# A mixture-of-experts kernel: the experts' second matrix laid out and loaded as 96 rows instead of 88

## The chip, the cores and the metric

The kernel runs on one core of a Trainium2 chip. The metric is the time of one launch on the device, in microseconds (us), the median of several runs. The core has a matrix engine (PE; its weight loads are shown apart as PEld), a vector engine (DVE), a scalar engine (ACT), a general engine (POOL), an engine that here only issues DMA transfers (SP), and 16 DMA engines that carry all transfers.

## What is computed

Two layers, each attention and then a feed-forward part, with a layer norm after each, over 2 x 1024 tokens of 256 features in fp32. The change touches only the last part, a mixture of experts. Cut to this part, the reference is:

```
E, I, K = (64, 176, 6)
router_logits = x @ gate_w.T
probs = jax.nn.softmax(router_logits, axis=-1)
topk_w, topk_idx = jax.lax.top_k(probs, K)
topk_w = topk_w / jnp.sum(topk_w, axis=-1, keepdims=True)
combine = jnp.sum(jax.nn.one_hot(topk_idx, E, dtype=x.dtype) * topk_w[..., None], axis=1)
h = jax.nn.silu(jnp.einsum('th,eih->tei', x, experts_w1))
y = jnp.einsum('tei,ehi->teh', h, experts_w2)
routed_out = jnp.einsum('teh,te->th', y, combine)
```

A shared expert is added to `routed_out`, and the layer norm closes the kernel. Every token goes to 6 of 64 experts. Each expert has a first matrix of 256 x 176 and a second of 176 x 256.

## The kernel before

The routed work is sorted by expert: 2048 x 6 = 12288 rows, in 96 tiles of 128 rows (FULL). A tile may hold rows of several experts, so the loop of `experts` runs over 159 pairs of a tile and an expert (STEPS = 96 + 63). The router (`route`) works out, on the chip, the token of every row (`tok_i`), its place in the output (`dst_i`), and the expert and tile of each step (`owner`).

Step b does the following:

- SP loads the expert's number with a value load (L1848), waits until the step five earlier has finished with the buffer (`y_made`), and issues two transfers: the first matrix into `w1` (L1850), 128 rows of 1408 bytes, and the second into `w2` (L1851), 88 rows of 2048 bytes. There are B = 5 buffers of each. The profile calls the buffers `moe_w`; two of the five `w2` lie in a tile named `keep_prod`, and show under that name.
- POOL gathers the rows of tile b + 6 from memory (L1869, as long as there are tiles), and from step 64 on scatters a finished tile of outputs (L1874). Both are indirect transfers of 128 rows of 1 KB.
- PE transposes a gathered tile (`turn`, L1901), multiplies it by the first matrix (`up`, L1912: eight matmul instructions a step), and multiplies the result of the step before by the second (`down`, L1921: four instructions).
- ACT copies the transposed tile (L1952, L1960) and applies SiLU to the first product (L1966), and DVE adds the second product to the tile's sum under a mask (L2010).

The second product has an inner size of 2 x 88. It is taken as 2 x 96 (HPAD): PE reads 96 rows of `ht` (the SiLU's result) and of `w2`, and the rows 88 to 95 of both must hold zeros. POOL therefore clears the two `ht` and the five `w2` buffers once, in the router's stage (L1603), and counts them on the semaphore `padded`; SP waits for all seven clears ahead of its first weight load (L1560), PE and ACT at the start of the experts stage. Each transfer then writes rows 0 to 87 only.

The first five steps' matrices are loaded in the router's stage (L1563, L1565), as soon as SP has fetched the list of experts. At the end of the kernel the outputs are read back from memory, weighed and added up, and normalised.

In memory, `lay_out` stores each expert's second matrix as 88 rows of 512 floats (the two halves of the inner dimension side by side).

Of the kernel before, what the change touches and what calls it, by code (L numbers as in the profile page):

```python
# [19 lines left out]
KT = E // P  # L20
# [1432 lines left out]
HALF = WIDE // 2  # L1453
HPAD = 96
# [8 lines left out]
B, RB, LEAD = 5, 9, 6  # L1463
# [6 lines left out]
def route(nc, a, keep):  # L1470


    with ExitStack() as ctx:
# [75 lines left out]
        @block.sync  # L1549
        def _(sp):  # L1550
            sp.dma_start(w_up[:], a["w_sh_up"].rearrange("(k p) n -> p k n", p=P)).then_inc(sh_in, 16)
            for m, width in enumerate(SH_TILES):
                sp.dma_start(w_down[0:width, m], a["w_sh_down"][m * P:m * P + width]).then_inc(sh_in, 16)
            sp.dma_start(a["x_rows"].rearrange("(t p) n -> p t n", p=P), x[:]).then_inc(x_out, 16)
            sp.wait_ge(owned, 1)
            sp.dma_start(a["owners"].rearrange("(j p a) -> p j a", p=P, j=2), owner_i[:]).then_inc(owner_out, 16)
            sp.wait_ge(owner_out, 16)
            sp.dma_start(owner[:], a["owners"].rearrange("(o n) -> o n", o=1)).then_inc(owner_in, 16)
            sp.wait_ge(owner_in, 16)
            sp.wait_ge(keep["padded"], 2 + B)  # L1560
            for b in range(B):
                e = sp.value_load(owner[0:1, b:b + 1], min_val=0, max_val=EXPERTS - 1)
                sp.dma_start(keep["w1"][b][:], a["w1"][e].rearrange("p (k j n) -> p k j n", k=KT, j=2)  # L1563
                             ).then_inc(keep["w_in"][b], 16)
                sp.dma_start(keep["w2"][b][0:HALF], a["w2"][e].rearrange("p (j n) -> p j n", j=2)  # L1565
                             ).then_inc(keep["w_in"][b], 16)
            sp.wait_ge(x_out, 16)

        @block.gpsimd
        def _(pool):  # L1570
            done = 0

            def ordered(instruction):

                nonlocal done
                instruction.then_inc(consts, 1)
                done += 1
                pool.wait_ge(consts, done)

            ordered(pool.iota(iota[:], pattern=[[1, TILES]], base=0, channel_multiplier=0,  # L1580
                              allow_small_or_imprecise_dtypes=True))
            ordered(pool.iota(lane[:], pattern=[[1, 1]], base=0, channel_multiplier=1,
                              allow_small_or_imprecise_dtypes=True))
            ordered(pool.iota(tile_no[:], pattern=[[1, 2]], base=0, channel_multiplier=2,
                              allow_small_or_imprecise_dtypes=True))
            ordered(pool.memset(ones[:], 1.0))
            ordered(pool.memset(ones_f[:], 1.0))
            ordered(pool.memset(zeros[:], 0.0))
            ordered(pool.iota(token[:], pattern=[[P, NT]], base=1, channel_multiplier=1,
                              allow_small_or_imprecise_dtypes=True))  # L1590
            ordered(pool.iota(k_rows[:], pattern=[[TOK, TOP - 1]], base=0, channel_multiplier=0,
                              allow_small_or_imprecise_dtypes=True))
            ordered(pool.memset(before[:], 1.0))
            ordered(pool.memset(below[:], 1.0))
            ordered(pool.affine_select(out=before[:], in_=before[:], compare_op=ALU.is_gt, fill=0.0,
                                       base=0, pattern=[[1, P]], channel_multiplier=-1))
            ordered(pool.affine_select(out=below[:, 0], in_=below[:, 0], compare_op=ALU.is_gt, fill=0.0,
                                       base=0, pattern=[[1, EXPERTS]], channel_multiplier=-1))
            ordered(pool.affine_select(out=below[:, 1], in_=below[:, 1], compare_op=ALU.is_ge, fill=0.0,
                                       base=0, pattern=[[1, EXPERTS]], channel_multiplier=-1))  # L1600
            ordered(pool.memset(sums[:, 0], 0.0))
            for m in keep["ht"] + keep["w2"]:
                pool.memset(m[:], 0.0).then_inc(keep["padded"], 1)  # L1603
            for n in range(UNITS):
                width = SH_TILES[n % ST]
                pool.wait_ge(silu, n + 1)
                pool.wait_ge(u_in, n + 1)
                pool.tensor_tensor(sh_h[n // ST][0:width, n % ST], sh_gate[n % 2][0:width], sh_up[n % 2][0:width],
                                   ALU.mult).then_inc(fuse, 1)
            pool.wait_ge(split, 1)  # L1610
            for n, (t, k) in list(enumerate(pairs))[1::2]:
                if n >= HOTS:
                    pool.wait_ge(hot_used, n - HOTS + 1)
                pool.tensor_scalar(hot_low[:, n % HOTS], iota[:, 0:P], low[:, t, k:k + 1], None,
                                   ALU.is_equal).then_inc(hot_low_in, 1)
            pool.wait_ge(x_out, 16)
            pool.wait_ge(tok_in, 1)
            for t in range(LEAD):
                pool.indirect_dma_start(keep["rows"][t], None, a["x_rows"], bass.IndirectOffsetOnAxis(
                    ap=tok_i[:, t:t + 1], axis=0)).then_inc(keep["rows_in"][t], 16)  # L1620
# [186 lines left out]
def experts(nc, a, keep):  # L1807

    with ExitStack() as ctx:
# [4 lines left out]
        w1, w2, rows_all, rows, ht = (keep[n] for n in ("w1", "w2", "rows_all", "rows", "ht"))  # L1814
        w_in, rows_in, padded = (keep[n] for n in ("w_in", "rows_in", "padded"))
# [28 lines left out]
        @block.sync  # L1844
        def _(sp):
            for b in range(B, STEPS):
                n = b % B
                e = sp.value_load(owner[0:1, b:b + 1], min_val=0, max_val=EXPERTS - 1)  # L1848
                sp.wait_ge(y_made, b - B + 1)
                sp.dma_start(w1[n][:], a["w1"][e].rearrange("p (k j n) -> p k j n", k=KT, j=2)).then_inc(w_in[n], 16)  # L1850
                sp.dma_start(w2[n][0:HALF], a["w2"][e].rearrange("p (j n) -> p j n", j=2)).then_inc(w_in[n], 16)  # L1851
            for n in range(B):
                sp.wait_ge(w_in[n], 32 * len(range(n, STEPS, B)))
            sp.wait_ge(xt_in, STEPS)
            for n in range(YB):
                sp.wait_ge(y_out[n], 16 * len(range(n, FULL, YB)))
            for t in range(NT):
                sp.dma_start(got[t], a["y_rows"].rearrange("(k t p) n -> t p k n", k=TOP, p=P)[t]).then_inc(got_in[t], 16)
            for a0, a1 in NORM:
                sp.wait_ge(norm["normed"], a1)  # L1860
                sp.dma_start(a["out"].rearrange("(t p) n -> p t n", p=P)[:, a0:a1], x[:, a0:a1]).then_inc(stored, 16)
            sp.wait_ge(stored, 16 * len(NORM))
# [28 lines left out]

        @block.tensor
        def _(pe):
            pe.wait_ge(padded, 2 + B)

            def turn(t):
                pe.wait_ge(rows_in[t % RB], 16 * (t // RB + 1))
# [49 lines left out]
        def _(act):  # L1947
            def keep_tile(t):
                act.wait_ge(turned, t + 1)
                if t >= RING:  # L1950
                    act.wait_ge(xt_in, t - RING + EXPERTS)
                act.activation(tiles[:, t % RING], xt_ps[t % 2][:, 0:KT * P].rearrange("p (k t) -> p k t", k=KT),  # L1952
                               ACT.Copy).then_inc(tile_in, 1)
# [12 lines left out]
                act.activation(ht[b % 2][0:HALF], h_ps[b % 2][0:HALF, 0:2 * P].rearrange(  # L1966
                    "p (j t) -> p j t", j=2), ACT.Silu).then_inc(h_in, 1)

            act.wait_ge(padded, 2 + B)
            keep_tile(0)  # L1970
            take_tile(0)
            keep_tile(1)
# [140 lines left out]
def lay_out(i):  # L2113
# [3 lines left out]
    d = {}  # L2117
# [13 lines left out]
    for n, k in enumerate(("w_q1", "w_k1", "w_v1")):  # L2131
# [6 lines left out]
    w1, w2 = t(np.asarray(i["L1_ffn_experts_w1"])), t(np.asarray(i["L1_ffn_experts_w2"]))  # L2138
    rows = lambda w, k: np.ascontiguousarray(w.reshape(EXPERTS, k, w.shape[1] // k, w.shape[2]).transpose(
        0, 2, 1, 3).reshape(EXPERTS, w.shape[1] // k, k * w.shape[2]))  # L2140
    d["w1"], d["w2"] = rows(w1, KT), rows(w2, 2)
    d["w_sh_up"], d["w_sh_down"] = t(np.asarray(i["L1_ffn_shared_gate_up"])), t(np.asarray(i["L1_ffn_shared_down"]))
    return d

# [23 lines left out]
```

## Time and profile before

| | |
|---|---|
| median of 3 runs | 1293.59 us (1291.06 to 1298.01) |
| the profiled execution | 1297.3 us, its span 1295.6 us |
| PE busy | 1128.8 us (87% of the span) |
| DVE, ACT, POOL busy | 825.3, 633.3, 592.2 us |
| DMA | 137.21 MB, a mean of 106 GB/s |
| expert loop | from 910 to 1239 us |

PE's busy share alone says little here: the profile also shows what each engine waited for, the chain of waits that ended last, and, for any stretch, the mean busy share of the 16 DMA engines and the rate that they moved. A mean share below 1 can come from 16 engines that are all partly idle, or from some that are full beside others that are empty.

### The profile page before, as it was taken

To read this page: it belongs to the slowest core of one execution; us is meant where nothing else is said; L and a number is where in the kernel's file an instruction comes from. 1 tells how busy PE (TensorE), PEld (TensorE's weight loads), DVE (VectorE), ACT (ScalarE), POOL (GpSimd) and SP (SyncE) were. 2 spreads that over 40 slices of the span, in tenths; PEclk is the share of its full clock that TensorE was granted. 3 is DMA by queue.
4 is the path that set the end of the run, shared out by engine and by line. 5 is a ranking of instruction groups with operands and counts; after the bars stand their busy time and mean duration, and the time that the engine had idled before them with its cause. 6 is when DMAs were issued, how large, how long until landed. Compare 5 with 4: busy or idle time off the path is not lost. (4 is left out here: it accounts for less than half of the span.)

```text
span 1295.6 us, 21119 instructions
## 1 busy us (share of the span) xinstructions
PE 1128.8 (87%) x6374; PEld 660.5 (51%) x6374; DVE 825.3 (64%) x1537; ACT 633.3 (49%) x1320; POOL 592.2 (46%) x589
## 2 busy tenths in 40 slices
PE   5489999999999995888898977897999998999965
PEld 2152222222222223455753556356888886788854
DVE  6399999999999945665454556897333333222246
ACT  1126777777777781455313342221555554444471
POOL 7000355667345363576541102458544457555521
PEclk8888999999999997999989997899899999999989
DMA  4990234234130104000000000210689888788877
GB/s 135 152 228 14 47 59 64 28 41 61 27 44 13 13 9 171 0 2 1 1 3 1 1 1 10 89 56 26 197 242 242 238 238 252 241 267 255 261 253 253
DMA packets 128383, 137.21 MB, mean 106 GB/s; under 512 B 47430, under 2 KB 99366, under 8 KB 128207
## 3 DMA queue, kind: packets, MB, share of 16 engines
q1 hardware_dynamic: 118783, 110.42, 34.2%
q0 software_dynamic: 9216, 25.18, 6.1%
q8 instruction: 53, 0.87, 0.3%
q14 instruction: 59, 0.48, 0.1%
q10 hardware_dynamic: 272, 0.26, 0.1%
HBM read 109.06 MB, written 24.12 MB: 103 GB/s over the span
## 5 line engine op out<-in xcount | busy, mean ns | idle before, releaser
L495 ACT ACTIVATE l_ret_store<-attn_st 128x512 f32<-128x512 f32 x512 | 280.1, 598 | 103.1 <-PE attn_st L406 93.3
L519 DVE TENSOR_REDUCE attn_neg<-attn_mx 128x8 f32<-128x1024 f32 x256 | 299.2, 1202 | 12.9 <-PE attn_mx L386 11.9
L2010 DVE SCALAR_TENSOR_TENSOR exp_sums<-exp_y_ps,moe_mask,exp_sums 128x256 f32 x159 | 77.0, 484 | 202.8 <-PE exp_y_ps L1921 97.3
L406 PE MATMUL attn_st<-attn_q_st,attn_k_st 128*128 128x512 bf16 x512 | 173.9, 384 | 2.8 <-ACT l_ret_store L495 2.1
L1912 PE MATMUL exp_h_ps<-keep_prod,moe_w 128*88 128x128 f32 x1272 | 169.9, 277 | 7.1 <-DMA moe_w<-in_w 5.2
L386 PE MATMUL attn_mx<-attn_k_st,attn_q_st 96*128 96x512 bf16 x512 | 156.2, 387 | 14.5 <-DVE attn_neg L519 14.2
L1912 PEld LDWEIGHTS exp_h_ps<-keep_prod,moe_w 128*88 128x88 f32 x1272 | 147.8, 158 | 23.6 <-DMA moe_w<-in_w 12.2
L418 PE MATMUL attn_o<-l_ret_store,l_ret_tab 128*32 128x512 f32 x1024 | 136.4, 604 | 0.8 <-ACT l_ret_store L495 0.8
L1874 POOL DMA_INDIRECT y_rows<-exp_sums,moe_dst_i x96 | 93.7, 976 | 82.9 <-DVE exp_sums L2010 75.6
L406 PEld LDWEIGHTS attn_st<-attn_q_st,attn_k_st 128*128 128x128 bf16 x512 | 48.3, 97 | 155.9 <-ACT l_ret_store L495 114.6
L1966 ACT ACTIVATE moe_ht<-exp_h_ps 88x256 f32<-88x256 f32 x159 | 60.4, 380 | 95.6 <-PE exp_h_ps L1912 95.5
L278 POOL CAST attn_neg_parts<-attn_neg 128x128 bf16<-128x128 f32 x16 | 4.6, 289 | 210.5 <-DVE attn_neg L519 210.5
L1921 PE MATMUL exp_y_ps<-moe_w,moe_ht 96*128 96x256 f32 x380 | 97.6, 379 | 0.0
L1960 ACT ACTIVATE keep_prod<-exp_tiles 128x256 f32 x159 | 66.2, 416 | 60.2 <-issue 59.6
L1869 POOL DMA_INDIRECT moe_rows<-x_rows,moe_tok_i x70 | 66.6, 952 | 58.6 <-PE exp_xt_ps L1901 49.3
L386 PEld LDWEIGHTS attn_mx<-attn_k_st,attn_q_st 96*128 96x128 bf16 x512 | 48.9, 99 | 67.5 <-DVE attn_neg L519 28.7
L1921 PEld LDWEIGHTS exp_y_ps<-moe_w,moe_ht 96*128 96x128 f32 x380 | 64.6, 190 | 5.2
L1921 PE MATMUL exp_y_ps<-keep_prod,moe_ht 96*128 96x256 f32 x256 | 66.1, 380 | 0.0
L354 PE MATMUL attn_st<-keep_x_t,l0b_front 128*128 128x512 f32 x64 | 36.8, 735 | 32.9 <-DVE l0b_front L505 25.7
L535 DVE STREAM_TRANSPOSE l0b_pv_t<-attn_o 128x512 f32<-128x512 f32 x64 | 45.0, 703 | 12.9 <-PE attn_o L418 12.7
L535 DVE STREAM_TRANSPOSE keep_x_t<-attn_o 128x512 f32<-128x512 f32 x64 | 45.0, 703 | 6.9 <-PE attn_o L418 6.8
L1998 DVE MEMSET exp_sums<- 128x256 f32 x96 | 26.1, 272 | 34.5 <-DVE exp_sums L2010 25.7
(317 smaller groups left out, 1921.0 us busy)
## 6 DMA issues: line engine op xcount, KB each, us to landing
moe_w<-in_w SPq DMA_DIRECT2D x254, 176.0 KB
keep_prod<-in_w SPq DMA_DIRECT2D x64, 176.0 KB
exp_tiles<-y_rows SPq DMA_DIRECT2D x11, 768.0 KB, 10.3
parts<-l0b_front SPq DMA_DIRECT2D x32, 192.0 KB, 10.6
attn_k_st<-parts SPq DMA_DIRECT2D x48, 128.0 KB, 7.1
attn_q_st<-parts SPq DMA_DIRECT2D x48, 128.0 KB, 7.7
l_ret_tab<-in_tables SPq DMA_DIRECT2D x4, 1024.0 KB
exp_sums<-y_rows SPq DMA_DIRECT2D x5, 768.0 KB, 10.5
```

Source lines behind the costliest of these rows:

```text
L386: mm = pe.matmul(bank[:, half * CH:(half + 1) * CH], q, k_st[g % BUFS][0:STACK, h, half * CH:(half + 1) * CH], start=True, stop=True)
L406: pe.matmul(st_ps[n % BANKS][:], k_st[g % BUFS][:, h, kt * P:(kt + 1) * P], q_st[g % BUFS][:, h, c * CH:(c + 1) * CH], start=True, stop=Tr ...
L418: mm = pe.matmul(o_ps[32 * h:32 * h + 32, :], v_st[:, b, kt, head + h], probs[s % 2][:, h], start=True, stop=True)
L495: act.activation(probs[s % 2][:, h], st_ps[n % BANKS][:], ACT.Exp, scale=SCALE0).then_inc(exp_done, 1)
L519: dve.tensor_reduce(neg[m % 2][:, i], mx_ps[slot["score", n] % 2][:].rearrange("p (j k) -> p j k", k=P), AX.X, ALU.max, negate=True).then_ ...
L535: dve.transpose(pv_t[u % 2][:, kt].rearrange("p n d -> p (n d)"), o_ps[:]).then_inc(pv_kept, 1)
L1869: pool.indirect_dma_start(rows[t % RB], None, a["x_rows"], bass.IndirectOffsetOnAxis(ap=tok_i[:, t:t + 1], axis=0)).then_inc(rows_in[t % R ...
L1874: pool.indirect_dma_start(a["y_rows"], bass.IndirectOffsetOnAxis(ap=dst_i[:, t:t + 1], axis=0), sums[:, t % RING], None).then_inc(y_out[t ...
L1912: mm = pe.matmul(h_ps[b % 2][0:HALF, j * P:(j + 1) * P], w1[n][:, k, j], xt[b % XB][:, 0, k], start=(k == 0), stop=(k == KT - 1))
L1921: mm = pe.matmul(y_ps[b % 2][:, 0:E], ht[b % 2][:, j], w2[b % B][:, j], start=(j == 0), stop=(j == 1))
L1960: act.activation(xt[b % XB][:], tiles[:, bass.ds(at, 1)], ACT.Copy).then_inc(xt_in, 1)
L2010: dve.scalar_tensor_tensor(out=sums[:, bass.ds(at, 1)], in0=y_ps[b % 2][:, 0:E].unsqueeze(1), scalar=mask[:, b:b + 1], in1=sums[:, bass.ds ...
```

## The change

The second matrix is laid out in memory with 96 rows per expert, of which the last eight are zeros, and each transfer writes all 96 rows of its buffer. The clears of the `w2` buffers go, and with them SP's wait for `padded`; PE and ACT wait for two clears instead of seven.

```diff
@@ route, block.sync
             sp.wait_ge(owner_in, 16)
-            sp.wait_ge(keep["padded"], 2 + B)
             for b in range(B):
                 e = sp.value_load(owner[0:1, b:b + 1], min_val=0, max_val=EXPERTS - 1)
                 sp.dma_start(keep["w1"][b][:], a["w1"][e].rearrange("p (k j n) -> p k j n", k=KT, j=2)
                              ).then_inc(keep["w_in"][b], 16)
-                sp.dma_start(keep["w2"][b][0:HALF], a["w2"][e].rearrange("p (j n) -> p j n", j=2)
+                sp.dma_start(keep["w2"][b][:], a["w2"][e].rearrange("p (j n) -> p j n", j=2)
                              ).then_inc(keep["w_in"][b], 16)
@@ route, block.gpsimd
-            for m in keep["ht"] + keep["w2"]:
+            for m in keep["ht"]:
                 pool.memset(m[:], 0.0).then_inc(keep["padded"], 1)
@@ experts, block.sync
-                sp.dma_start(w2[n][0:HALF], a["w2"][e].rearrange("p (j n) -> p j n", j=2)).then_inc(w_in[n], 16)
+                sp.dma_start(w2[n][:], a["w2"][e].rearrange("p (j n) -> p j n", j=2)).then_inc(w_in[n], 16)
@@ experts, block.tensor
-            pe.wait_ge(padded, 2 + B)
+            pe.wait_ge(padded, 2)
@@ experts, block.scalar
-            act.wait_ge(padded, 2 + B)
+            act.wait_ge(padded, 2)
@@ lay_out
-    d["w1"], d["w2"] = rows(w1, KT), rows(w2, 2)
+    d["w1"], d["w2"] = rows(w1, KT), np.pad(rows(w2, 2), ((0, 0), (0, HPAD - HALF), (0, 0)))
```

## Rows read from the trace of the kernel before

**Rows 1.** The page: GB/s moved in 40 equal slices of the span.

```profile
GB/s 135 152 228 14 47 59 64 28 41 61 27 44 13 13 9 171 0 2 1 1 3 1 1 1 10 89 56 26 197 242 242 238 238 252 241 267 255 261 253 253
```

**Rows 2.** Timeline, PE: starts of steps 3, 69, 70, 93, 94, 158.

```profile
917.18 1.03 PE L1912 MATMUL exp_h_ps<-keep_prod,moe_w 128*88 128x128 f32 x8
...
1051.46 1.03 PE L1912 MATMUL exp_h_ps<-keep_prod,moe_w 128*88 128x128 f32 x8
1053.42 1.03 PE L1912 MATMUL exp_h_ps<-keep_prod,moe_w 128*88 128x128 f32 x8
...
1113.05 1.04 PE L1912 MATMUL exp_h_ps<-keep_prod,moe_w 128*88 128x128 f32 x8
1114.79 1.04 PE L1912 MATMUL exp_h_ps<-keep_prod,moe_w 128*88 128x128 f32 x8
...
1236.16 1.11 PE L1912 MATMUL exp_h_ps<-keep_prod,moe_w 128*88 128x128 f32 x8
```

**Rows 3.** The chain of waits by line, of 909 to 1053, then 1123 to 1236.

```profile
by line: PE exp_h_ps L1912 38.4%; PE exp_y_ps L1921 34.3%; DMA moe_w<-in_w 12.4%; PE exp_xt_ps L1901 8.4%; SPq L1850 1.8%; issue 1.6%; SPq L1848 1.5%; SPq L1851 1.3%; ACT keep_prod L1960 0.3%; ACTq L1956 0.2%; ACTq L1960 0.0%
...
by line: SPq L1848 26.7%; SPq L1850 17.8%; SPq L1851 16.6%; issue 13.7%; DMA moe_w<-in_w 9.5%; PE exp_h_ps L1912 6.0%; PE exp_y_ps L1921 5.4%; DMA keep_prod<-in_w 4.5%
```

**Rows 4.** Timeline, POOL, of stretch B.

```profile
1076.71 0.97 POOL L1869 DMA_INDIRECT moe_rows<-x_rows,moe_tok_i  x1 [0.30 <-issue]
...
1079.28 0.97 POOL L1869 DMA_INDIRECT moe_rows<-x_rows,moe_tok_i  x1 [0.31 <-issue]
```

**Rows 5.** Waits (us, times, longest): PEld 909 to 1053; PEld, SP 1113 to 1237.

```profile
PEld exp_h_ps L1912 <- DMA moe_w<-in_w: 2.9, 6, 1.0
...
PEld exp_h_ps L1912 <- DMA moe_w<-in_w: 9.3, 16, 1.8
...
SPq L1850 <- PE exp_y_ps L1921: 2.4, 3, 1.2
```

**Rows 6.** Timeline, SP: first and fifth first-matrix issue of the preload.

```profile
845.06 0.40 SPq L1563 DMA_DIRECT2D moe_w<-in_w  x1
...
852.39 0.35 SPq L1563 DMA_DIRECT2D moe_w<-in_w  x1
```

**Rows 7.** SP's lines, 1113 to 1237 (ns min/median/max, first and last start); one issue.

```profile
L1850 SPq DMA_DIRECT2D moe_w<-in_w x62: 352/353/500, 1115.1 to 1231.7; - x62
...
L1851 SPq DMA_DIRECT2D moe_w<-in_w x38: 347/358/748, 1115.6 to 1232.2; - x38
...
L1848 SPq TENSOR_LOAD <-moe_owner x62: 486/504/882, 1112.8 to 1230.8; - x62
...
1164.75 0.75 SPq L1851 DMA_DIRECT2D moe_w<-in_w  x1
```

**Rows 8.** Short windows of the preload: last two columns DMA share and GB/s.

```profile
846.20:846.40 0.20, 0.20 (x1) 0.00 (x0) 0.20 (x1) 0.00 (x0) 0.00 (x0) 1.00 0.94 120
...
847.00:847.20 0.20, 0.20 (x2) 0.01 (x1) 0.20 (x1) 0.20 (x1) 0.00 (x0) 1.00 0.67 239
847.20:847.40 0.20, 0.20 (x2) 0.12 (x1) 0.20 (x1) 0.02 (x1) 0.04 (x1) 1.00 0.71 276
847.40:847.60 0.20, 0.20 (x2) 0.04 (x1) 0.20 (x1) 0.00 (x0) 0.20 (x1) 1.00 0.64 246
```

**Rows 9.** Windows among the 16-row loads, and in the tail.

```profile
307.00:308.00 1.00, 1.00 (x7) 0.30 (x5) 1.00 (x2) 0.89 (x3) 0.00 (x0) 1.00 1.16 125
...
1246.00:1252.00 6.00, 4.25 (x10) 3.47 (x11) 1.36 (x3) 6.00 (x22) 0.00 (x0) 0.50 1.09 358
```

**Rows 10.** Windows of stretches A and C, the same columns.

```profile
940.00:1050.00 110.00, 108.69 (x756) 97.12 (x755) 40.69 (x108) 61.62 (x162) 46.94 (x51) 1.00 0.87 238
1123.00:1233.00 110.00, 104.73 (x693) 89.83 (x692) 27.74 (x58) 45.86 (x116) 56.12 (x58) 1.00 0.83 259
```

**Rows 11.** Clears on POOL (timeline), and POOL's next line (groups, 800 to 830).

```profile
812.65 1.53 POOL L1603 MEMSET moe_w<- 96x512 f32 x3
...
L1608 POOL TENSOR_TENSOR route_sh_h<-route_sh_gate,route_sh_up 128x512 f32<-128x512 f32 (+1 forms) x3 | 5.1, 1716 | 9.2 <-ACT route_sh_up L1695 9.2
```

## The prediction

> **What bounds the kernel now.** The change touches only the mixture-of-experts part. The page's slices place it: the expert loop is the block at 197 to 267 GB/s at the end (slices 28 to 38 of 40, counted from 0) [rows 1]. How fast its steps go is read from the start of each step's first matmul [rows 2]. They fall into three stretches:
>
> - A, steps 3 to 70 (917.18 to 1053.42): 136.2 us. A step in which nothing is late takes 1.96 us (1051.46 to 1053.42), so 67 of them are 131.3 us, and 4.9 us are lost.
> - B, steps 70 to 93 (to 1113.05): 59.6 us, against 45.1 at 1.96.
> - C, steps 93 to 158 (to 1236.16): 123.1 us. Nothing is left to transpose, an undisturbed step is 1.74 us (1113.05 to 1114.79), 65 of them are 113.1, and 10.0 us are lost.
>
> The chain of waits, cut to A and to C [rows 3], says by what. In A it is mostly PE itself (81% with the transposes), with 12% on weight transfers. In C it is SP: L1848, L1850 and L1851 hold 61%, weight transfers 14%. B is POOL's: each tile costs it a gather and a scatter, 2.57 us from one gather to the next (1076.71 to 1079.28) [rows 4]. The waits [rows 5] agree: PE's weight loads stood 2.9 us for `moe_w` in A and 9.3 in C, while in C SP itself waited only 2.4 us for PE. SP is late there by its own work, and it has a pace of its own: in the preload, where nothing but its value loads and issues run, 845.06 to 852.39 is four steps, 1.83 us each [rows 6]. That is more than PE's 1.74, so C cannot get down to PE's pace.
>
> But SP is slower than that in C: 61 steps from 1115.1 to 1231.7 are 116.6 us [rows 7], where 1.83 would give 111.6. 5.0 us are lost on SP's queue. The row at 1164.75 shows one kind of loss: the issue of a second matrix takes 0.75 us, where the median is 0.36. I read that as a push back from full DMA queues.
>
> **How full the queues are.** The view of short windows over the preload [rows 8] matters most. While the first matrix (128 rows) is moving, the mean share of the 16 DMA engines is 0.94 (846.2). By 847.0 it has landed (its issue was at 845.06, and the next first matrix is issued one SP step later, about 846.9, and moves about 1 us after that), and only the second (88 rows) is moving: the share stands at 0.67, 0.71, 0.64, at 239 to 276 GB/s. 11/16 is 0.69, and 88 is 11 x 8. So the 88-row load sits on 11 engines, 8 rows each, and 5 stand idle. Is a load always 8 rows per engine? No: twelve loads of 16 rows each (L177, L179) queue up from 303 us, and the share in a window among them is 1.16 [rows 9], so there one row per engine is used. What fits 128, 88 and 16 is the largest number up to 16 that divides the rows; 96 = 16 x 6 would then use all 16.
>
> The Trainium skill, "DMA: Bandwidth & Descriptors", section "Why a DMA increments its semaphore by 16 and not by 1", says the same: the number of engines is the largest up to 16 that divides the slowest dimension of both sides, and a 96-partition tile is named as a case of 16. The trace agrees on 88 rows (0.64 to 0.71); a 96-row load by itself is not seen in it.
>
> The load in engine-microseconds: the windows 847.0 to 847.6 hold a share sum of 2.02, times 0.2 us times 16 = 6.5 for 152 KB, so the 180 KB of the second matrix (88 x 512 x 4 bytes) cost 7.7. On 11 engines this is 0.70 us each. With 96 rows it is 8.4, on 16 engines 0.53 us each.
>
> In A the share is 0.87 [rows 10] over a mean step of 2.03 us, 28.3 engine-us. Less 7.7 leaves 20.6, or 1.29 on every engine. So the 11 carry 1.99 of 2.03 us (98%), the other five 1.29 (63%). After: (20.6 + 8.4)/16 = 1.81 us, 92% of 1.96.
> In C (share 0.83, step 1.89): 25.1, less 7.7, is 1.09 each; the 11 carry 1.79 of 1.89 (95%), the five 58%. After: 25.8/16 = 1.61, 88% of SP's 1.83.
> So the busiest engines are nearly full now, and get 9 to 10% less work, though the bytes rise.
>
> **The change part by part.**
> - Five clears removed from POOL, 2.5 us in all (the last three 1.53 us, ended by 814.2) [rows 11]. They lie beside the router's work: POOL's next instruction, L1608, still stood idle for ACT's results, 9.2 us before its first three. Worth 0. If that cover were gone, 2.5 us.
> - SP's wait on `padded` removed: the clears had ended at 814.2, SP issues its preload from 845.06, held by the owner list [rows 6]. Worth 0. PE's and ACT's waits for it come 90 us later still: 0. The two clears of `ht` stay.
> - 159 transfers of 96 rows instead of 88, 16 KB more each, 2.6 MB. What an issue of 96 rows costs SP isn't shown, but one of 128 rows takes 353 ns and one of 88 takes 358 [rows 7]; between them it is nothing. Even 5 ns over 65 steps would be 0.3 us.
> - PE's work is the same: it read 96 rows before too.
> - The even spread, in A: it can return at most 4.9 us. The stalls there are a few steps whose weights were late behind queues at 98%. At 92% most of these go. I take 3.5 (0 to 4.9).
> - In B POOL sets the pace, and its two issues don't get shorter. Only the landing of the last gathered tile can come a little sooner, once: 0.5 (-0.5 to 1.5).
> - In C the ceiling is SP's own pace: 5.0 us of its queue, and the last load lands perhaps 0.5 us sooner; PE now starts its last step 4.5 us after SP's last first-matrix issue [rows 2, 7]. 2.4 of the 5.0 is waiting for a PE that had itself stalled for weights, and goes with those stalls. I take 4.7 (0 to 6). What is late next is SP, with its value load and two issues.
> - After 1239 us nothing changes: the loads of the tail fetch other data.
>
> Sum: 3.5 + 0.5 + 4.7 = 8.7 us. The profiled execution took 1297.3 us (span 1295.6), so 1288.6 of its kind; the median of the runs is 1293.59, 3.7 below it, so 1284.9.
>
> **The rivals.**
> - *The total rate, not the busiest engine, is the limit (slower).* If all traffic can't go faster than the 238 GB/s of A and 259 of C, 16.4 KB more on some 490 KB a step cost 3.3% of both: 0.033 x 259 us = 8.6 us slower, 1302. It decides once the rate needed, 508 KB per 1.96 us = 259 GB/s in A or per 1.83 us = 278 in C, can't be had. Against it: the tail moves 358 GB/s for 6 us [rows 9]. For it: those are other row sizes, and no slice of the expert loop is over 267.
> - *The queues never delayed SP and PE (no change).* The late weights come from a slow memory answer now and then, and SP's long steps from its value loads (486 to 882 ns) [rows 7]. Then the saving is 0 to 3 us: 1292. For it: in A PE mostly runs at 1.96 though 11 engines are at 98%. Against: a random delay needs slack to be swallowed, and a shorter queue is slack.
> - *96 rows go to 12 engines.* The change then spreads nothing (8 rows on the busiest, as now) and adds a little: 1294. The 16-row loads speak against it. I count it into the case of no change.
> - *All of it comes back.* 4.9 + 1.5 + 6 = 12.4: 1281. For it: five engines were idle some 40% of the time.
>
> **How the numbers follow.** My forecast (a gain of 6 to 11 us, 1283 to 1288) 0.42; all of it back 0.18; no change in any of its forms (a gain of 0 to 6) 0.31; slower by total rate 0.09. 0.5% is 6.5 us, about what a measurement of this kernel can tell from no change. Faster by more: nearly all of the forecast and the full return, 0.57. Slower by more: 0.07. Within: 0.36. The range for 8 in 10 goes from the full return, with 3 us for the play of the median, 1278, to the case of no change, with 1.5 us above it, 1295.
>
> **What the profile after would show.** No clear of `moe_w` or `keep_prod` on POOL. In the preload windows a share near 0.95 during the second matrix instead of 0.69, and that phase near 0.55 us. In C SP's first-matrix issues 1.83 to 1.85 us apart, its 61 steps 112 us; the waits of PE's weight loads for `moe_w` in C below 4 us instead of 9.3, in A below 1. B unchanged. The forecast is wrong if the share in the preload stays at 0.69 or goes to 0.75; or if it rises but the transfers get slower (C's share at 0.9 or more, no more than 265 GB/s); or if SP's steps stay at 1.9 us though the engines have room.

## The result

The changed kernel takes 1285.1 us (median of 20 runs, 1280.68 to 1294.51), beside 1294.27 us for the kernel before (20 runs, 1287.31 to 1300.59): a ratio of 0.994, with a 95% interval of 0.9922 to 0.9958, or 5 to 10 us saved. The profiled execution took 1285.45 us, its span 1283.7.

### The profile after

Timeline, PE, the starts of steps 3, 70, 93, 94, 95 and 158, to be held against [rows 2]; all lines are numbered one lower than before:

```profile
911.31 0.93 PE L1911 MATMUL exp_h_ps<-keep_prod,moe_w 128*88 128x128 f32 x7
...
1045.80 0.38 PE L1911 MATMUL exp_h_ps<-keep_prod,moe_w 128*88 128x128 f32 x2
...
1104.93 1.24 PE L1911 MATMUL exp_h_ps<-keep_prod,moe_w 128*88 128x128 f32 x8
1107.67 1.72 PE L1911 MATMUL exp_h_ps<-keep_prod,moe_w 128*88 128x128 f32 x8
1110.09 1.04 PE L1911 MATMUL exp_h_ps<-keep_prod,moe_w 128*88 128x128 f32 x8
...
1224.08 1.04 PE L1911 MATMUL exp_h_ps<-keep_prod,moe_w 128*88 128x128 f32 x8
```

| stretch | before | after | saved | forecast |
|---|---|---|---|---|
| A, steps 3 to 70 | 136.2 | 134.5 | 1.7 | 3.5 |
| B, steps 70 to 93 | 59.6 | 59.1 | 0.5 | 0.5 |
| C, steps 93 to 158 | 123.1 | 119.2 | 3.9 | 4.7 |

The first two steps of C took 2.74 and 2.42 us after, instead of 1.74. The granted clock was 0.72 on the mean from 1104 to 1110, and 0.50, the lower of TensorE's two levels (1.2 GHz), from 1106 to 1109; PE had done nothing from 1103 to 1104. So C is also given from step 95 on: 119.6 before and 114.0 after. The two spans differ by 11.9 us, more than the runs do: the loop starts 5.1 us earlier after (904.92 instead of 909.98), which is not the change's doing: in the profiles of the other versions below it starts anywhere from 901.93 to 910.90. From its first step to its last the loop took 326.2 us before and 319.2 after. Each of these stretches comes from one profile.

The chain of waits, of 904 to 1046 and then of 1115 to 1224, to be held against [rows 3]:

```profile
by line: PE exp_h_ps L1911 38.7%; PE exp_y_ps L1920 35.6%; DMA moe_w<-in_w 12.2%; PE exp_xt_ps L1900 8.9%; issue 1.6%; SPq L1849 0.9%; POOL y_rows L1873 0.7%; POOL moe_rows L1868 0.7%; DVE exp_sums L2009 0.3%; ACT keep_prod L1959 0.3%; SPq 
...
by line: PE exp_h_ps L1911 39.4%; PE exp_y_ps L1920 37.8%; DMA moe_w<-in_w 9.2%; DMA keep_prod<-in_w 4.8%; SPq L1849 2.7%; issue 2.4%; SPq L1847 2.0%; SPq L1850 1.9%
```

A looks as before. In C SP has gone from 61% of the chain to 7%, and PE from 11% to 77%. The reason is in SP's timeline of the preload (compare [rows 6]) and in SP's lines of C (compare [rows 7]; L1847 is the value load, L1849 and L1850 the two issues):

```profile
839.45 0.40 SPq L1562 DMA_DIRECT2D moe_w<-in_w  x1
...
846.03 0.34 SPq L1562 DMA_DIRECT2D moe_w<-in_w  x1
...
L1849 SPq DMA_DIRECT2D moe_w<-in_w x62: 347/348/357, 1108.1 to 1219.2; - x62
...
L1850 SPq DMA_DIRECT2D moe_w<-in_w x38: 332/333/1077, 1108.6 to 1219.7; - x38
...
L1847 SPq TENSOR_LOAD <-moe_owner x62: 263/272/715, 1104.0 to 1218.4; - x62
```

846.03 less 839.45 is four of SP's own steps, the pace at which SP goes when nothing holds it up: 1.645 us each; before they were 1.833. The issues are hardly shorter (353 and 358 ns before). The value load is: 272 ns instead of 504. SP's own step is now below PE's 1.74, so C goes mostly at PE's pace; the steps from 95 on still took 4.4 us more than 63 times 1.74. An issue of L1850 still takes up to 1.08 us now and then. Such long issues, which the forecast read as a push back from full queues, have not become fewer: in C three of them took over 0.5 us before, and five after.

The spread over more engines is there. Short windows of the preload, while the second matrix moves (compare [rows 8]), and windows of A and C (compare [rows 10]; the last two columns are the mean share of the 16 DMA engines and GB/s):

```profile
841.40:841.60 0.20, 0.20 (x2) 0.13 (x1) 0.20 (x1) 0.20 (x1) 0.00 (x0) 1.00 0.86 314
841.60:841.80 0.20, 0.20 (x2) 0.00 (x1) 0.20 (x1) 0.14 (x1) 0.00 (x0) 1.00 0.94 369
...
940.00:1050.00 110.00, 108.65 (x767) 98.54 (x766) 41.31 (x110) 62.64 (x165) 51.39 (x54) 1.00 0.99 255
...
1123.00:1220.00 97.00, 94.95 (x642) 83.79 (x641) 25.79 (x54) 42.28 (x107) 51.40 (x54) 1.00 0.92 282
```

The share while 96 rows move is 0.86 to 0.94, where 88 rows held 0.64 to 0.71, and the rate is up to 369 GB/s. The number of engines can also be counted. The page of a run gives the packets of the queue that carries these loads, here of the kernel before, of the changed kernel and of two runs that follow, rows90 and rows128:

```profile
q1 hardware_dynamic: 118783, 110.42, 34.2%
...
q1 hardware_dynamic: 120850, 113.02, 36.5%
...
q1 hardware_dynamic: 119737, 111.07, 34.2%
...
q1 hardware_dynamic: 125938, 123.44, 36.4%
```

The changed kernel has 2067 packets more, which is 13 for each of the 159 loads: 8 for the added rows and 5 others. rows90 has 954 more, 6 a load: 2 rows and 4 others. rows128 has 7155 more, 45 a load: 40 rows and 5 others. One small packet for each engine that takes part fits all three, with 11 engines at 88 rows, 15 at 90, and 16 at 96 and 128.

In the loop the share did not fall as forecast: it is 0.99 in A and 0.92 in C. It can't be read as how full the engines are, though. It was above 1 in [rows 9], and it is 1.04 over 100 us of A in split_after, a version below.

So two things changed at once, the number of engines that share the load and SP's own step, and the experiments had to tell them apart.

### The profile page after: what moved, and what is told of

It reads as the page before. It is cut to its first block and busy times, and to the rows that moved or that the text cites. A ratio compares the mean times of both kernels' runs of the same rounds, so it can differ in the third digit from the quotient of the medians.

```text
span 1283.7 us, 21272 instructions
## 1 busy us (share of the span) xinstructions
PE 1117.6 (87%) x6374; PEld 657.9 (51%) x6374; DVE 825.5 (64%) x1537; ACT 633.0 (49%) x1320; POOL 589.9 (46%) x584
```

## The experiments

Every ratio is to the kernel before, run along with it. In the first set, the first four, the kernel before took 1315.73 us, in the later ones 1293.27 and 1292.86; nothing here shows why. In the profiles of the first set stretch B is also some 11 to 13 us longer, so only ratios compare between the sets. SP's own step is read from the preload, C from PE's timeline (steps 95 to 158; 63 steps at 1.74 are 109.6 us), both from one profile of each version.

| version | SP's own step, us | C, us | ratio (95%) |
|---|---|---|---|
| before | 1.833 | 119.6 | 1 |
| changed | 1.645 | 114.0 | 0.994 (0.9922 to 0.9958) |
| clears_kept | 1.648 | 116.7 | 0.9931 (0.9906 to 0.9956) |
| rows88 | 1.892 | 127.2 | 1.0033 (1.001 to 1.0055) |
| rows90 | 1.923 | 129.5 | 1.0025 (1.0 to 1.005) |
| rows128 | 1.647 | 115.9 | 0.9926 (0.9897 to 0.9954) |
| slow_sp | 1.645, and one more value load in every third step of the loop | 121.3 | 1.0008 (0.9983 to 1.0033) |
| before_fixed | 0.812 | 112.2 | 0.9939 (0.991 to 0.9968) |
| after_fixed | 0.925 | 110.4 | 0.9908 (0.9872 to 0.9945) |
| swap_before | 1.770 | 116.8 | 0.9982 (0.9958 to 1.0006) |
| swap_after | 1.635 | 113.6 | 0.9955 (0.9926 to 0.9983) |
| split_before | 1.833 | 118.5 | 0.999 (0.9971 to 1.001) |
| split_after | 1.645 | 111.4 | 0.9918 (0.9886 to 0.995) |
| split_after2 | 1.645 | 110.3 | 0.9906 (0.988 to 0.9933) |

### The clears alone

```diff
-            for m in keep["ht"]:
+            for m in keep["ht"] + keep["w2"]:
```
(and the three waits for `2 + B` again)

> The changed kernel (96 rows per load) with the five clears and all waits for seven clears put back. If the clears and waits are worth nothing, as forecast, it stands where the changed kernel stands, 0.994 of the time before (within 0.3%). If they were on a path, it loses up to 2.5 us of the gain: 0.996.

0.9931, no worse than the changed kernel. The clears and the waits for them were worth nothing that the runs can tell. This run also is the 96-row reference of the first set.

### The number of rows

In rows88 and rows90, with the clears kept, the buffers and the layout have 96 rows and a load takes the first n of them:

```diff
-                sp.dma_start(w2[n][:], a["w2"][e].rearrange("p (j n) -> p j n", j=2)).then_inc(w_in[n], 16)
+                sp.dma_start(w2[n][0:90], a["w2"][e][0:90].rearrange("p (j n) -> p j n", j=2)).then_inc(w_in[n], 16)
```

In rows128 buffers and layout have 128 rows, all are loaded, and PE reads the first 96:

```diff
-    d["w1"], d["w2"] = rows(w1, KT), np.pad(rows(w2, 2), ((0, 0), (0, HPAD - HALF), (0, 0)))
+    d["w1"], d["w2"] = rows(w1, KT), np.pad(rows(w2, 2), ((0, 0), (0, P - HALF), (0, 0)))
```

> As the first, but each load takes rows 0 to 87 of the 96-row layout: the loads of before, only the distance from one expert to the next in memory is new. Theory of the load's shape (11 engines, 8 rows each): as before, 1.000, SP's steps in the preload 1.83 us. Rival, the new layout in memory helps: 0.994 again.

> As the first, but each load takes 90 rows, which 15 engines can share at 6 rows each. The profile after shows two changes at once: an even spread, and SP's own step in the preload of 1.62 us where it was 1.83. Theory that the spread made the gain: the busiest engines carry 6 rows as with 96, so 0.994 to 0.995. Theory that SP's shorter step made it in stretch C, and that this comes only with all 16 engines: SP's preload step is 1.83 us again, C is SP-bound and only A's 2.5 us remain: 0.998. DMA share in the preload about 0.94 while the second matrix moves.

> The changed kernel with 128 rows per load (40 of them zeros): 16 engines at 8 rows each, so the busiest engine carries what it did before, while SP's step should be the short one, 1.62 us. Bytes per step 573 KB instead of 492. Theory of the spread: DMA engine time of 1.8 us and more per step on all 16, as much as the 11 had before, so no gain or a loss: 1.000 to 1.006. Theory of SP's step: C keeps its 5.6 us, 0.996. If the total rate is a limit below 300 GB/s: slower still, 1.01 and more.

rows88 is back at the kernel before, a little above it: the gain is not the new layout's. (In the new layout each second issue starts 0.07 us later on SP, which adds to its step.)

rows90 and rows128 go against the theory of the spread. With 90 rows the load is spread, 6 rows on each of 15 engines, and nothing is gained: 1.0025, where the theories had 0.994 and 0.998. SP's own step did not stay at 1.83 us there but rose to 1.92, and that could hide a small gain of the spread. rows128 has no such flaw. With 128 rows the busiest engine carries 8 rows, as before, every step moves 573 KB, and the whole gain is there: 0.9926, beside the 0.9931 of clears_kept with 96 rows. SP's value loads in the preload, of rows90 and of rows128, and windows of A and C of rows128:

```profile
L1562 SPq TENSOR_LOAD <-moe_owner x5: 475/480/488, 843.6 to 851.3; - x5
```

```profile
L1561 SPq TENSOR_LOAD <-moe_owner x5: 264/273/482, 844.3 to 851.2; - x5
```

```profile
940.00:1040.00 100.00, 99.05 (x707) 90.67 (x706) 38.07 (x101) 57.61 (x151) 45.34 (x48) 1.00 0.92 291
1145.00:1240.00 95.00, 91.97 (x622) 81.53 (x621) 25.16 (x52) 41.12 (x104) 49.59 (x53) 1.00 0.96 313
```

The gain goes with the short value load (273 ns at the median; the 482 ns are the first of the five, ahead of any weight load), and this with 16 engines. rows128 also settles the forecast's slower rival: at 313 GB/s the loop is not held up by the total rate.

The Trainium skill ("DMA: Bandwidth & Descriptors", "Why a DMA increments its semaphore by 16 and not by 1") says that for a load on k < 16 engines the issuing sequencer itself writes the remaining 16 - k counts of the semaphore. It gives no price for this chip. That SP pays something for k < 16 agrees with these rows; that this write is what SP pays for, no run here shows.

### SP's step by itself

slow_sp keeps the 96-row loads and makes SP slower:

```diff
                 n = b % B
+                if b % 3 == 0:
+                    sp.value_load(owner[0:1, b:b + 1], min_val=0, max_val=EXPERTS - 1)
                 e = sp.value_load(owner[0:1, b:b + 1], min_val=0, max_val=EXPERTS - 1)
```

before_fixed and after_fixed take SP's value loads out of the kernel before and of the changed kernel:

```diff
-                e = sp.value_load(owner[0:1, b:b + 1], min_val=0, max_val=EXPERTS - 1)
+                e = b * EXPERTS // STEPS
```

> The changed kernel with one more value load on SP in every third step of the expert loop (its result is not used). A value load with its register work takes some 0.7 us, so SP's own step grows from 1.64 to about 1.88 us on the mean, what the 88-row and the 90-row loads need, while the transfers stay those of the changed kernel. Theory that SP's step makes the difference: the gain is gone, 1.000 to 1.003. Theory that all 16 engines carrying the load make it in some other way (landing sooner, shorter queues): 0.993 to 0.995, as the changed kernel.

> The kernel before with the value loads of SP left out: the number of the expert whose matrices a step loads is written into the program (step x 64 / 159) and no longer read from the router's list, so the wrong expert's matrices may be used; transfers, sizes and waits are those of before. SP's own step falls to about 1.1 us. Theory of SP's step: as fast as the changed kernel or faster, 0.990 to 0.994, by way of C, where PE's 1.74 us becomes the pace. Theory of the spread: the 11 engines are as full as before, 0.998 to 1.000.

> The same edit in the changed kernel: no value loads on SP, fixed expert numbers, 96 rows. Against the run before it this shows what the spread is worth when SP's step can't matter. Theory of SP's step: the same as the 88-row version within 0.2%. Theory of the spread: 0.3% or more below it.

The last two leave out the reading of the expert's number, so they multiply by the wrong experts' matrices in places; transfers and sizes are the same.

slow_sp, with the spread of the changed kernel and 16 engines, has no gain left: 1.0008. The extra value load cost a little less than expected: in C, SP's steps took 2.27 us at the median with it and 1.63 and 1.65 without, 1.85 on the mean, which is about the 1.83 of the kernel before. So at the old pace of SP the spread alone gives nothing that the runs can tell. before_fixed, with 88 rows on 11 engines, has all of the gain: 0.9939. SP's own step fell there to 0.81 us, further than the expected 1.1 and than the change brought it. Windows of A and C of before_fixed:

```profile
940.00:1040.00 100.00, 98.00 (x694) 89.11 (x693) 37.28 (x99) 56.44 (x148) 42.97 (x46) 1.00 0.87 239
1125.00:1210.00 85.00, 84.20 (x575) 75.94 (x573) 23.20 (x48) 38.13 (x96) 46.42 (x49) 1.00 0.87 277
```

With 11 engines for the second matrix C moves 277 GB/s and goes at 1.78 us a step. By the forecast's reckoning these engines were 95% full at 259 GB/s and were what held C up; they were not.

after_fixed, at 0.9908, is 0.3% below before_fixed. That is just the mark that had been set for the spread being worth something once SP is out of the way, and the profiles lean that way too (A, steps 3 to 68, 131.3 and 130.2 us; C 112.2 and 110.4). But the intervals overlap, so the runs neither show such a share of 0.3% nor rule it out.

### Where on SP the 0.2 us lies

```diff
-                sp.dma_start(w1[n][:], a["w1"][e].rearrange("p (k j n) -> p k j n", k=KT, j=2)).then_inc(w_in[n], 16)
                 sp.dma_start(w2[n][0:HALF], a["w2"][e].rearrange("p (j n) -> p j n", j=2)).then_inc(w_in[n], 16)
+                sp.dma_start(w1[n][:], a["w1"][e].rearrange("p (k j n) -> p k j n", k=KT, j=2)).then_inc(w_in[n], 16)
```
(swap_before; swap_after is the same in the changed kernel)

> The kernel before with its two issues of a step in the other order: the second matrix (88 rows) first, then the first matrix (128 rows). In the profiles SP's value load takes 496 ns behind an 88-row issue and 475 to 488 behind a 90-row one, but 275 ns behind one of 96 or 128 rows. Theory that a value load is slow only when the issue just before it used fewer than 16 engines: here it follows 128 rows, takes about 275 ns, SP's preload step is 1.61 to 1.65 us, and the kernel gains what the change gains, 0.993 to 0.995, with 88 rows and the old layout. Rival, every issue on fewer engines costs SP 0.2 us wherever it stands: the preload step stays at 1.83 us and the ratio at 1.000.

> Control: the changed kernel (96 rows) with the same swap. Both issues use 16 engines, so SP's step stays at 1.64 us in either theory, and the order of landing doesn't matter as the first product waits for both: 0.993 to 0.995.

My theory here, that a value load is slow only straight behind an issue on fewer than 16 engines, fell; it had the step at 1.61 to 1.65 us and the ratio at 0.993 to 0.995. SP's value load in swap_before, where a 128-row issue stands before it, and in swap_after, which with 0.9955 (0.9926 to 0.9983) isn't told from the changed kernel:

```profile
L1848 SPq TENSOR_LOAD <-moe_owner x154: 437/467/904, 900.7 to 1219.9; - x154
```

```profile
L1847 SPq TENSOR_LOAD <-moe_owner x154: 262/270/800, 901.4 to 1217.8; - x154
```

467 ns at the median of the loop, where the kernel before has 514 over the same loop (in the preload 466 and 496), though the 88-row issue now lies one issue further back. SP's own step is 1.77, still a little above PE's 1.74, and the ratio 0.9982 fits it, though its interval reaches 1. Of the engines that load such values it is SP alone that pays. The value loads of ACT (L1956) and DVE (L2003) from the same tile, in the kernel before and, after the break, in the changed kernel (L1955, L2002):

```profile
L1956 ACTq TENSOR_LOAD <-moe_owner x159: 273/282/725, 908.6 to 1233.6; - x159
L2003 DVEq TENSOR_LOAD <-moe_owner x159: 298/304/735, 907.7 to 1238.4; - x159
```

```profile
L1955 ACTq TENSOR_LOAD <-moe_owner x159: 272/282/692, 903.5 to 1221.7; - x159
L2002 DVEq TENSOR_LOAD <-moe_owner x159: 299/304/554, 902.6 to 1226.2; - x159
```

They are the same in both. What in SP makes its value load 0.2 us longer stays open.

### Slack for the second matrix

PE's first product of a step waited for both matrices, though it reads only the first. With a semaphore for each:

```diff
 def up(b):
-                pe.wait_ge(w_in[n], 32 * (b // B + 1))
+                pe.wait_ge(w_in[n], 16 * (b // B + 1))
 def down(b):
+                pe.wait_ge(w2_in[b % B], 16 * (b // B + 1))
                 pe.wait_ge(h_in, b + 1)
```
(and the second matrices' transfers count on `w2_in` instead of `w_in`)

> The changed kernel with a semaphore of its own for the second matrices: the first product of a step no longer waits for the second matrix, which is needed only after the first product. The second matrix is issued and lands last, so it gets about 1 us more of slack for nothing. If the stalls that remain (2.4 us in A, 4.3 us in C by the profile after) are weights late by less than that, most go: 0.989 to 0.991. If they are late first matrices, 0.994.

> The kernel before with a semaphore of its own for the second matrices, as was tried in the changed kernel (0.9918). It gives PE slack, but SP's own step stays 1.83 us: C stays near SP's pace, 65 steps of 1.83 us, and only A's stalls and the slack go. 0.996 to 0.998. If slack alone were what is missing: 0.992.

> The changed kernel with the semaphore of its own a second time, since its first result, 0.9918 (0.9886 to 0.995), doesn't tell it from the changed kernel's 0.994. Expected again 0.990 to 0.993; by the profile its loop is 314.5 us where the changed kernel's was 319.2.

In the changed kernel it gives 0.9918 and 0.9906, in the kernel before 0.999, less than the 0.996 to 0.998 expected. The waits of PE's weight loads for the first product, from 904 to 1224 in the changed kernel and, after it, in split_after2:

```profile
PEld exp_h_ps L1911 <- DMA moe_w<-in_w: 8.1, 18, 1.8
...
PEld exp_h_ps L1911 <- DMA keep_prod<-in_w: 1.9, 6, 0.7
```

```profile
PEld exp_h_ps L1912 <- DMA moe_w<-in_w: 2.4, 7, 0.8
```

10.0 us of waits become 2.4 (4.5 in split_after), and C is 110.3 us, 0.7 above PE's own pace. In the kernel before, the same edit leaves SP with 61% of the chain of C, as it was, and the runs don't tell it from no change. The split in the changed kernel is the best version found that uses the right experts: both of its intervals lie below 1, and it is 0.2 to 0.3% below the changed kernel, though the intervals overlap; its loop is 314.5 and 313.3 us by the profiles, where the changed kernel's was 319.2.

## Why the forecast came out right, and what was wrong in it

The time was right, 1284.9 forecast and 1285.1 measured, and so was the order of the stretches: C gave most, then A, then B. The cause of most of the gain was not the one forecast. That the time met to 0.2 us is luck: the interval of the gain alone goes from 5 to 10 us, and by the profiles the stretches gave 6.1 us, or the whole loop 7.0, where 8.7 were reckoned. The term of C came near because something that the sum had fixed, SP's own step, fell.

- *Clears and waits worth nothing*: right. In the profile the five clears are gone, and with them kept the ratio is 0.9931.
- *96 rows use 16 engines*: right, by the packets and by a share of 0.86 to 0.94 in the preload windows instead of 0.64 to 0.71.
- *The busiest engines get 9 to 10% less work, and this gives the time back*: this step failed. First its sums: A was to stand at 92% and stands at 99% (0.99 x 16 x 2.01 us, A's mean step, is 31.8 engine-us, where 29.0 were reckoned); C was to stand at 88% and stands at 92%. The share that these sums took for fullness is not a measure of it: rows128 moves 573 KB a step at a share of only 0.92 in A. Then its effect: slow_sp has the spread and no gain, rows128 and before_fixed have the old load on the busiest engine and the whole gain. What may be left for it is the 0.3% between before_fixed and after_fixed, which is not shown.
- *An issue of 96 rows costs SP what the others cost, "between them it is nothing"*: this was the mistake. I compared the durations of the issue instructions themselves, 353 and 358 ns, and these are indeed alike. The price stands in another row of the same view, the value load: 504 ns before, 272 after. So SP's own step, which I had taken as a floor of 1.83 us for C, was not one: it is 1.645 now. [rows 7] showed the 504 ns, but nothing there to hold it against; the value loads of ACT and DVE, 282 and 304 ns in the same trace, would have been that, and I didn't look.
- *In C, 5.0 us of push back come back*: 4.7 were forecast for C and the size was about right (3.9 from step 93, 5.6 from 95), the cause not. The long issues still occur, up to 1.08 us. SP's 61 steps took 111.1 us (1108.1 to 1219.2) where 112 were forecast, and 100 would be its own pace now: PE sets them.
- *A, 3.5 us*: 1.7, half of it. The chain there still has 12% of weight transfers, as before, and PE's weight loads waited 2.4 us for `moe_w` instead of 2.9, where less than 1 was forecast. In C they waited 5.6 instead of 9.3, where less than 4 was.
- *B, 0.5 us*: 0.5.
- *The tail unchanged*: 59.6 us from the last step to the end of the span, 59.4 before.
- *Slower, as the total rate is the limit*: refuted, by 282 GB/s in C after and by 313 with 128 rows.
- *No change, as queues were never what delayed*: half right. The load on the queues was not what mattered, but the time moved by another way.

## What to carry to other kernels

On an engine that issues transfers in a tight loop, reckon its own step from a place where it runs unhindered, and compare every instruction in it with its like on other engines before taking it as a floor. A load of more rows can cost the issuing engine less around the issue than a smaller one: with 96 or 128 rows instead of 88 SP's own step was 0.19 us shorter here. It pays only where that engine, or the slack behind it, sets the pace. And let a consumer wait only for the operand that it reads first: a semaphore of its own for the later operand seems to have given another 0.2 to 0.3%, beside the 0.6% of the change itself.

## What the runs showed of the hardware that I had not expected

- SP's value load takes 466 to 519 ns at the median in each kernel that loads 88 or 90 rows a step, and 267 to 275 ns in each that loads 96 or 128. ACT's and DVE's don't change with it (278 to 284, and 304 to 305).
- Loads on 11 engines beside loads on 16 reach 277 GB/s in the loop at a mean share of 0.87; with all on 16, 313 GB/s.
- What an 88-row load on 11 engines costs the loop by the transfers themselves is too little for these runs to show (0.3% between before_fixed and after_fixed, whose intervals overlap).
- A mean share of the DMA engines above 1 is possible over 100 us (1.04), so a share near 1 doesn't say that they have no room.
